# Second attention of a two-layer transformer: scores computed a second time with keys on partitions, in place of turning the exponentials

## The reference

```python
xn = adaln(x, c, g1, w_ada1, b_ada1)
qkv = bitlinear(xn, w_qkv, b_qkv).reshape(B, T, 3, H, hd)
q, k, v = (qkv[:, :, i].transpose(0, 2, 1, 3) for i in range(3))
attn = jax.nn.softmax(jnp.einsum('bhqd,bhkd->bhqk', q, k) * hd ** (-0.5), axis=-1)
o = jnp.einsum('bhqk,bhkd->bhqd', attn, v).transpose(0, 2, 1, 3).reshape(B, T, D)
x = x + bitlinear(o, w_proj, b_proj)
```

## Time and profile before

| what | value |
|---|---|
| median of 3 runs | 4012.81 us |
| profiled execution | 4011.16 us |
| its span, first to last instruction | 4009.4 us |
| mean granted TensorE clock | 0.973 of full speed |
| PE / DVE / ACT / POOL busy | 94% / 68% / 67% / 26% of the span |
| attention 1, first product to the store of the last heads | 2557.6 to 3633.1 us |

### The profile page before, as it was taken

How to read it: one execution, slowest core, us unless ns; L and a number is a source line. 1 busy time by engine, 2 the same in 40 slices (tenths; PEclk the granted TensorE clock), 3 DMA queues, 4 the chain that set the end, 5 groups by cost and what they waited for, 6 DMA issues and landing times. The chain is left out here.

```text
span 4009.4 us, 70221 instructions
## 1 busy us (share of the span) xinstructions
PE 3775.5 (94%) x26756; PEld 2543.0 (63%) x26756; DVE 2721.6 (68%) x4863; ACT 2687.9 (67%) x4667; POOL 1035.5 (26%) x1544
## 2 busy tenths in 40 slices
PE   8997999999999986999999959799999999995999
PEld 7885666666666664778888835466666666662555
DVE  4335888888888876444421148688888888885987
ACT  2226888888888854222222238688888888884998
POOL 0004555555555465000000037100000000002554
PEclk9998999999999998999999979899999999997999
DMA  5446233333333088244531038733332333313221
GB/s 189 184 164 152 62 67 62 67 62 67 62 67 62 14 285 272 100 137 158 176 114 53 32 131 303 205 62 67 62 67 62 67 61 67 62 30 127 77 80 51
DMA packets 307567, 419.53 MB, mean 105 GB/s; under 512 B 89449, under 2 KB 165741, under 8 KB 307227
## 3 DMA queue, kind: packets, MB, share of 16 engines
q1 hardware_dynamic: 307232, 415.03, 36.8%
HBM read 257.34 MB, written 157.32 MB: 103 GB/s over the span
## 5 line engine op out<-in xcount | busy, mean ns | idle before, releaser
L555 ACT ACTIVATE Sn<-Sn,mn 128x1024 f32<-128x1024 f32 x1024 | 1174.8, 1147 | 30.4 <-DVE mn L583 19.0
L521 PEld LDWEIGHTS pt<-ident,Sn 128*128 128x128 f32 x8192 | 881.2, 141 | 420.8 <-issue 413.5
L521 PE MATMUL pt<-ident,Sn 128*128 128x128 f32 x8192 | 1123.4, 280 | 1.0 <-DVE PT L547 0.4
L545 ACT ACTIVATE PT<-pt 128x512 f32<-128x512 f32 x1280 | 738.2, 597 | 236.0 <-PE pt L521 235.9
L489 PE MATMUL sp<-KS,QS 97*128 97x512 f32 (+1 forms) x2048 | 733.6, 440 | 45.3 <-DMA KS<-s_khi 23.6
L583 DVE CUSTOM_DVE_ANT_0 Sn<-sp,biastile 128x1024 f32<-128x1024 f32 x512 | 624.4, 1220 | 145.1 <-PE sp L489 113.5
L585 DVE TENSOR_SCALAR_CACHE_REDUCE Sn<-sp 128x1024 f32<-128x1024 f32 x512 | 624.3, 1220 | 137.3 <-PE sp L489 137.3
L628 POOL TENSOR_SCALAR biastile<-dist,ascale 128x1024 f32<-128x1024 f32 x512 | 576.3, 1126 | 497.0 <-DVE mn L583 483.9
L510 PE MATMUL po<-PT,Vp 128*32 128x256 f32 x8192 | 651.4, 391 | 0.0
L547 DVE COPY PT<-pt 128x512 f32<-128x512 f32 x768 | 531.2, 692 | 118.5 <-PE pt L521 118.3
L1077 ACT ACTIVATE gf<-pf,b1T 128x512 f32<-128x512 f32 x128 | 88.3, 690 | 535.4 <-PE pf L1022 530.5
(11 more groups left out here) (237 smaller groups left out, 4985.8 us busy)
## 6 DMA issues: line engine op xcount, KB each, us to landing
QS<-s_qhi SPq DMA_DIRECT2D x128, 256.0 KB, 5.0
KS<-s_khi SPq DMA_DIRECT2D x128, 256.0 KB, 7.2
KS<-s_klo SPq DMA_DIRECT2D x64, 256.0 KB, 6.1
QS<-s_qlo SPq DMA_DIRECT2D x64, 256.0 KB, 6.9
Vp<-s_v SPq DMA_DIRECT2D x64, 256.0 KB, 7.8
s_o<-og SPq DMA_DIRECT2D x32, 512.0 KB, 8.7
xA<-in_x SPq DMA_DIRECT2D x8, 1024.0 KB, 5.7
s_qhi<-qstage SPq DMA_DIRECT2D x32, 256.0 KB, 2.0
```

Source lines behind the costliest of these rows:

```text
L521: op = nc.tensor.transpose(ps[:, i, :], sn[:, (g * HALF + i) * P:(g * HALF + i + 1) * P], K.ident[:])
L545: nc.scalar.activation(dst, src, ACT.Copy).then_inc(*s_cp_act.up())
L555: nc.scalar.activation(sn[:], sn[:], ACT.Exp, scale=-1.0, bias=mn[n % 3][:, t:t + 1], accum_out=sums[n % 5][:, t:t + 1]).then_inc(*s_exp.up())
```

## The change

`build_program` calls a new function `stage_attention1(K)` in place of `stage_attention(K, 1)`. The first attention keeps the old function. The new one goes by windows of two tiles (`w`, 256 windows and 15 more to drain; four windows are a head):

- `score` stays, but DVE only reduces it to the minimum (`minimum`, no copy to SBUF).
- The minima of a head are split in two float32r halves (`minima_halves`), PE turns them into two rows by eight float32 products (`minima_to_rows`), and ACT copies the two rows under the 96 rows of QS. KS has the constant -1 in the same two rows, written once by POOL.
- `score_turned(u-12)` computes the scores again with the keys as weights, over 98 rows, minus the minima, as two products of 128 x 512, each into one of two PSUM buffers `st1`.
- ACT takes exp of each half straight from PSUM into PT (`exponential`). There is no transpose and no copy of it.
- The row sums: POOL adds pairs of key blocks (`two`), DVE adds two of those (`four`), and PE multiplies by ones (`total`), twice for a head; ACT copies the result beside the copy of `po`, and PE turns both back (`turn_output`, four transposes).

The core of the diff:

```diff
+        ps_r = S.ps_ring("s1", 2, [P, L])
+        pst_r = S.ps_ring("st1", 2, [P, BLK])
+        po, psum = S.ps("po1", [P, QW]), S.ps("psum1", [P, QW])
...
+        def score_turned(u):
+            n, kb = divmod(u, LT)
...
+            for g in range(L // BLK):
+                ps = pst_r.take(pe, (u, g), (s_exp, 2 * u + g + 1))
+                nc.tensor.matmul(ps[:], ks[0:ROWS + 2, j, kb * P:(kb + 1) * P], qs[0:ROWS + 2, j, g * BLK:(g + 1) * BLK],
+                                 start=True, stop=True).then_inc(*s_st.up())
+
+        def minima_to_rows(n):
+            ps = ps_r.take(pe, ("row", n), (s_row, n + 1))
+            pe.wait_ge(s_mm, n + 1)
+            for t in range(LT):
+                op = nc.tensor.matmul(ps[ROWS:ROWS + 2, t * P:(t + 1) * P], mm[n % 2][:, t, :].bitcast(F32), K.ident[:], start=True, stop=True)
...
+        def times_v(u):
...
+            pe.wait_ge(s_exp, 2 * u + 2)
+            if kb == 0:
+                pe.wait_ge(s_ov, n)
...
+        def total(m):
...
+                op = nc.tensor.matmul(psum[g * HD:(g + 1) * HD, :], K.ones[:, 0:HD], four[m % 2][:, g * QW:(g + 1) * QW],
+                                      start=k == 0, stop=k == 1)
...
+        def tensor_program():
+            for w in range(NW + 15):
+                u = 2 * w
+                if u < N_TILES:
+                    score(u)
+                if 0 <= u - L_T < N_TILES:
+                    score_turned(u - L_T)
+                n, k = divmod(w - 14, 4)
+                if k == 0 and 0 <= n < N_HEADS:
+                    turn_output(n)
+                for x in (u - L_V, u - L_V + 1):
+                    if 0 <= x < N_TILES:
+                        times_v(x)
+                if w % 2 == 0 and 0 <= w // 2 - 5 < NW // 2:
+                    total(w // 2 - 5)
+                n, k = divmod(w - 4, 4)
+                if k == 0 and 0 <= n < N_HEADS:
+                    minima_to_rows(n)
+                if u < N_TILES:
+                    score(u + 1)
+                if 0 <= u - L_T < N_TILES:
+                    score_turned(u - L_T + 1)
...
+        def scalar_program():
+            for w in range(NW + 15):
+                x = 2 * w - L_T
+                for g in range(2):
+                    if 0 <= x < N_TILES:
+                        exponential(x, g)
+                n, k = divmod(w - 11, 4)
+                if k == 0 and 0 <= n < N_HEADS:
+                    act.wait_ge(s_pv, (n + 1) * LT)
...
+                    nc.scalar.activation(ov[n % 2][:, 0, :], po[:], ACT.Copy).then_inc(*s_ov.up())
...
+                for g in range(2):
+                    if 0 <= x < N_TILES:
+                        exponential(x + 1, g)
...
-        stage_attention(K, 1)
+        stage_attention1(K)
```

167 lines of the change are left out of this document (added).

## The result

The changed kernel takes 4260.84 us (median of 4 runs, 4258.34 to 4264.25) against 4012.74 for the kernel before, a ratio of 1.0617 with a 95% interval from 1.0599 to 1.0636. The forecast was 4139, with a range from 4050 to 4230. The sign was right, the size was not: 248 us lost instead of 126, and the time lies outside the range.

What follows compares the result with a forecast made beforehand. TensorE's own list was taken as the bound. Its work plus waits made 18.50 us a head; with fill and tail the stage took 1201 us against 1075.5, 126 more: 4139 us, own range 4085 to 4195, eight in ten 4050 to 4230.

Steps and rivals of the forecast that it cites:

- TensorE's own work: TensorE's products and transposes in the second attention, if it never waited: 15.4 us a head, 1.3 less than before.
- The two-buffer wait: Second turned product of each window waits for an exponential to free its PSUM buffer: 0.49 us, window 3.54.
- The wait for the copy of po: Next head's first product with V waits for ACT's copy, queued behind two exponentials: 1.02 us a head.
- The others have room: Other engines fit within the 18.50 us head: DVE 14.6, ACT 9.6, POOL 10.2 us.
- splitting 0.4: VectorE's splitting of the minima, counted as 0.4 us of its 14.6 us a head.
- The clock: Rival: TensorE's pauses lower its clock; a tenth of the stage at 1.2 GHz gives 4218 us; chance 0.10.
- Rival 1: Slower still, 4185 to 4250 us: exponentials at 0.69 us or the minima's weight loads laid bare; chance 0.18.
- the sixteen passes of the minima: Eight float32 products on TensorE, two passes each, turning the minima into rows: 1.70 us a head.
- Rival 3: Not slower: buffers free in time and the copy of po not waited for, 3937 us; chance 0.15.

Runs made afterwards that it cites:

- the last kernel: Changed kernel with all additions and minima splitting on GpSimd, minima rows a window later, three turned-score buffers, joint copy of po and sums placed earlier: 3968.3 us.
- e3: Changed kernel with only ACT's copy of po moved ahead of the exponentials of its window: 4190.4 us.
- e1: Changed kernel without GpSimd's additions; VectorE adds one pair of key blocks of four straight from PT, leaving half the keys out: 4155.4 us.
- e10_pool_writes_only: Changed kernel with GpSimd's addition replaced by filling the same tile with ones: 4170.6 us in one run.
- e2_spread: Changed kernel with the copy of po first and TensorE's order score, product with V, turned product for each tile: 4263.3 us.

## Why the prediction was wrong

**TensorE's own work: right.** The forecast's 15.4 us without waits became 15.72 in the last kernel, where TensorE is busy all the time; a head without the blocked VectorE is 18.51 where the clock is up, for 18.50.

**The two-buffer wait: right in size, not quite in form.** 3.57 for 3.54 us in a window with nothing else (e3), and 0.43 and 0.48 us gone with a third buffer in two windows. But I had one wait in a window, before the second turned product. The profile has one before each product of that pair, 0.3 to 0.4 us at the weight loads (510 in the stage). The window comes out as I had it.

**The wait for the copy of po: right.** 1.09 for 1.02, and gone with one move.

**"The others have room": the step that failed.** The forecast added VectorE's work up to 14.6 us a head, with each addition at "twice 0.92 (with POOL active)", and stopped there. Two things were wrong in it. The size: 0.92 was read as a slower rate, from a row whose instructions are 0.68 or 0.92. What the runs show is no rate but a wait until GpSimd's instruction ends. The trace of the kernel before had it already. In 27 of the row's 32 instructions GpSimd's addition of 1.27 us (L1863) is under way, with 0.3 to 0.4 us left, when VectorE's starts, and VectorE's ends 0.55 us after it; the other five take 0.68 to 0.69. Behind an addition of 2.36 us the same wait is up to 2.36. The place: I compared sums of work, not what is queued behind the blocked instruction. The 128 x 8 subtraction, within "splitting 0.4" in my sum, takes 2.2 us where it is blocked. With it and the additions VectorE has 8 x 1.22 + 2 x 2.57 + 2.4 + 0.8 = 18.1 us a head in place of 14.6. That would still fit into 20.3, but it falls late in windows where TensorE needs a PSUM slot or the minima. Cost: 1.60 us a head between the changed kernel and e1, 105 us in all. Without it the time would have been e1's 4155, inside the range.

**The clock: a rival that took part.** I gave 0.10 to it and priced a stretch at 0.96 of the clock at 31 us. That sum is wrong by itself: with levels of 1.2 and 2.4 GHz, 0.96 of the clock is 8% of the time at the lower one, and at my own 79 us for a tenth this is 63. In the changed kernel the clock was at 0.97, 68 us of the stage in 19 stretches. It cost much less than either price: 16 us in e1 by the difference of the means, about 5 in the changed kernel (20.36 for the mean, 20.29 for the four windows where the clock is up, times 64). With the one long wait gone it did not fall (e3).

**The rivals.** Rival 1 (longer exponentials or bare weight loads) did not happen: 0.597 us, and the sixteen passes of the minima take 1.84 (3100.70 to 3102.54) for my 1.70. Rival 3 (not slower) did not happen either. None of my cases had VectorE and GpSimd blocking each other, which is why the range ended at 4230.

The sum from 4139: 16 by the clock give e1's 4155, and 105 for GpSimd's and VectorE's shutting each other out give 4260. The 105 is itself the measured difference to e1, so only the 16 is a check of the sum.

## What to carry to other kernels

Before work goes to GpSimd, look at which VectorE instructions have two inputs in SBUF, or copy from SBUF to SBUF, and price each at its own time plus one whole GpSimd instruction, however small it is; then ask who waits behind it. An instruction that is 0.68 us in some places and 0.92 in others is not a slower one: look at what stands beside it on the other engine before you scale it up. And an engine's copy that another waits for belongs ahead of the long work of its window: one moved line was worth 70 us here.

## What the runs showed of the hardware that I had not expected

- VectorE's addition over two SBUF tiles takes 1.22 us alone, and ends 1.08 us after the end of a GpSimd addition that it meets. A 128 x 8 subtraction takes 0.17 us or, behind such an addition, 2.22 to 2.33. With GpSimd filling a tile instead, it takes 0.17 in the midst of the fill (e10_pool_writes_only, 48 times).
- A VectorE copy of 128 x 8 from SBUF to SBUF, with one input, took 1.98 us in the median in e2_spread and 1.33 in e3_copy_first, always up to the end of GpSimd's addition, and 0.17 where it did not meet one. VectorE's reductions out of PSUM kept their 1.22 us throughout, and its multiplication of a PSUM tile by an SBUF tile (128 x 128) its 0.28 to 0.29 us, 63 times during an addition of GpSimd's in the changed kernel.
- With a wait of 1.1 us once a head, TensorE's clock fell to 1.2 GHz 19 times in the stage, 18 of them within 0.1 us of the end of such a wait. Without that wait (e3_copy_first) it stayed at 1.00 over 900 us, although the weight loads still paused 0.3 to 0.4 us about twice in each window.
